# A layer with two long convolutions: PE's loop taken over groups 4 to 31, keys and values in one place each, fixed places for the second convolution's tiles

## What is computed

```
q, k, v = u Wq + bq, u Wk + bk, u Wv + bv          # per channel, over 512 positions
k  = causal_conv(k, k_kernel) + k_D * k            # first convolution, taps 512 long
kv = k * v
y  = causal_conv(kv, ssm_kernel) + D * kv          # second convolution
y  = (y * q) Wo + bo
x  = layernorm(u + y)
h  = square(relu(x W_fc));  d = h W_proj
s  = spikes of five steps of a leaky integrator driven by d, over 5
out = layernorm(x + s)
```

## Time and profile before

| | us |
|---|---|
| median of three runs | 869.58 |
| the profiled execution | 871.54 |
| its span | 869.4 |
| PE busy | 744.9 |
| DVE busy | 703.2 |
| ACT busy | 529.6 |
| POOL busy | 391.1 |

### The profile page before, as it was taken

The page is one execution under the profiler, slowest core; times in us unless marked ns, Lnnn a source line. Parts: engine busy times, 40 slices in busy tenths (PEclk is TensorE's granted clock), DMA queues, the critical chain, the costliest instruction groups (busy, mean ns, idle before and its releaser), DMA issues.

```text
span 869.4 us, 26708 instructions
## 1 busy us (share of the span) xinstructions
PE 744.9 (86%) x11392; PEld 547.4 (63%) x11392; DVE 703.2 (81%) x1100; ACT 529.6 (61%) x625; POOL 391.1 (45%) x307
## 2 busy tenths in 40 slices
PE   0068879999999798775499999999999999999993
PEld 0068879999999798775355555555555455555541
DVE  6896737877878757675569999999999999999885
ACT  2383748878877757665255556665556655566661
POOL 0332212223222212221475667866668766687542
PEclk9999969999999989776699999999999999999997
DMA  9994859999999867773000110011110111101001
GB/s 336 342 245 127 198 136 215 223 232 230 221 240 229 193 156 150 156 191 99 25 25 1 49 48 25 24 48 48 48 48 0 48 48 48 48 3 47 25 25 48
DMA packets 55580, 101.01 MB, mean 116 GB/s; under 512 B 5729, under 2 KB 41441, under 8 KB 53601
## 3 DMA queue, kind: packets, MB, share of 16 engines
q1 hardware_dynamic: 54144, 97.94, 43.9%
q10 hardware_dynamic: 1376, 2.23, 0.7%
HBM read 89.92 MB, written 27.01 MB: 134 GB/s over the span
## 4 chain that ended last, share of the span: by engine, by line
PE 44%; DVE 21%; POOL 17%; issue 11%; ACT 4%; DMA 1%; SPq 0%; POOLq 0%; DVEq 0%; ACTq 0%
PE ps L763 18%; POOL arena L687 14%; PE ps L741 13%; DVE arena L1238 7%; PE ps L874 5%; PE ps L881 5%; DVE u_maxima L975 2%; DVE arena L1195 2%; DVE arena L1235 2%; PE ps L855 2%; DVE arena L1214 2%; DVE arena L1220 2%; ACT arena L506 1%; PE ps L836 1%; DVE arena L1206 1%
## 5 line engine op out<-in xcount | busy, mean ns | idle before, releaser
L741 PE MATMUL ps<-arena 128*128 128x96 f16 x3072 | 143.3, 210 | 62.8 <-DVE arena L1028 51.1
L687 POOL TENSOR_TENSOR arena<-arena 128x512 f16<-128x512 f32 x128 | 178.6, 1426 | 14.9 <-ACT arena L570 14.3
L741 PEld LDWEIGHTS ps<-arena 128*128 128x128 f16 x3072 | 138.4, 100 | 64.7 <-issue 58.7
L881 PE MATMUL ps<-arena 128*128 128x512 f16 x768 | 173.2, 379 | 2.7 <-POOL arena L687 2.7
L874 PE MATMUL ps<-arena 128*128 128x512 f16 x768 | 170.8, 379 | 0.9 <-issue 0.9
L763 PE MATMUL ps<-arena 128*128 128x64 f16 (+2 forms) x5088 | 148.8, 184 | 25.9 <-issue 13.3
L763 PEld LDWEIGHTS ps<-arena 128*128 128x128 f16 x5088 | 145.4, 99 | 27.8 <-issue 20.7
L652 POOL TENSOR_TENSOR arena<-arena 128x512 f16<-128x512 f32 x32 | 37.8, 1182 | 245.3 <-ACT arena L526 245.3
L1227 DVE TENSOR_TENSOR arena<-arena 128x512 f32<-128x512 f32 x128 | 138.4, 1136 | 9.6 <-POOL arena L687 7.8
L566 ACT ACTIVATE arena<-ps,read_factor 128x512 f32<-128x512 f32 x128 | 88.0, 687 | 79.4 <-PE ps L874 62.7
L881 PEld LDWEIGHTS ps<-arena 128*128 128x128 f16 x768 | 73.9, 98 | 90.4 <-POOL arena L687 9.5
(11 more groups left out here) (108 smaller groups left out, 901.1 us busy)
## 6 DMA issues: line engine op xcount, KB each, us to landing
arena<-kpad_dram SPq DMA_DIRECT2D x166, 256.0 KB, 5.3
kpad_dram<-ksplit_dram SPq DMA_DIRECT2D x64, 256.0 KB, 6.1
qy<-in_uT SPq DMA_DIRECT2D x8, 1024.0 KB, 17.4
arena<-in_u SPq DMA_DIRECT2D x16, 512.0 KB, 4.1
out<-arena SPq DMA_DIRECT2D x16, 512.0 KB, 3.0
qy<-kpad_dram SPq DMA_DIRECT2D x22, 256.0 KB, 6.5
arena<-in_k SPq DMA_DIRECT2D x2, 512.0 KB, 4.8
ksplit_dram<-arena ACTq DMA_DIRECT2D x2, 512.0 KB, 3.3
```

Source lines behind the costliest of these rows:

```text
L687: nc.gpsimd.tensor_tensor(h16[:, 1, f], h_square[:, f % 4], h16[:, 0, f], ALU.subtract).then_inc(h_lo, 1)
L741: last = nc.tensor.matmul(o, u16[:, x, t, tok:tok + P], wcur[:, w, t], start=(k == 0), stop=(k == 3 * DT - 1))
L881: return nc.tensor.matmul(PD[:, t], wp16[:, w, f, t * P:(t + 1) * P], h16[:, h, f], start=first, stop=last)
```

## The change

The second convolution's windows get four fixed places, two halves for even and two for odd groups, in the same array as the first convolution's; `slot_of` and its table go. To make room, keys and values are kept in one 4 by 4 array of blocks each (quarter by group). A chunk is read out by group; a group's four blocks are free once it is used, and the same quarter of the next chunk is written into just these, transposed. So the chunks with even numbers are written into one contiguous run, and those with odd numbers into four separate blocks, by four instructions of 128 elements for the keys and four for the values in place of one of 512 each. kv gets a buffer of its own, `kv`, and is no longer stored over v; the factor that `times_v` applied moves into the reading of the values. The values may be written only after `times_v(g)` has used the block, so their reading moves behind it (`read_values`). The split keys have one buffer in place of two.

With places that depend on the parity of the group alone, PE's loop runs over the groups 4 to 31, fourteen iterations; an outer If leaves the projection out in the last two. The groups 0 to 3 and conv2(31) are written out. In the second phase `wo` and `bo_b` lie behind `yT`, and the staging area begins at 20 KB. The zeroing of the windows' upper partitions is regrouped: it is done before group 0 for all four places of the second convolution, and the separate memsets of before, for the query place, the token place and the late place, go.

```diff
         u16 = part(64, F16, "p (a t n) -> p a t n", a=2, t=DT)
-        kv_at = at[0]
-        kbuf = part(16, F32, "p (r q n) -> p r q n", r=2, q=GPC)
-        vbuf = part(16, F32, "p (r n) -> p r n", r=2)
+        kbuf = part(8, F32, "p (a b n) -> p a b n", a=GPC, b=GPC)
+        vbuf = part(8, F32, "p (a b n) -> p a b n", a=GPC, b=GPC)
+        kv = part(2, F32)
...
-        k16 = part(4, F16, "p (r a n) -> p r a n", r=2, a=2)
+        k16 = part(2, F16, "p (a n) -> p a n", a=2)
...
-        T = part(6 * 8, F16, "p (k c a n) -> p k c a n", k=6, c=HG, a=2)
-        at[0] = 48 * KB
-        T2 = part(2 * 8, F16, "p (k c a n) -> p k c a n", k=2, c=HG, a=2)
-        T3 = qy[:, (NC - 2) * CH * COL:].bitcast(F16).rearrange("p (k c a n) -> p k c a n", k=2, c=HG, a=2)
-        T4 = u16[:, :, :, 0:TOK // GPC].rearrange("p k t (c n) -> p k t c n", n=L)
-
-        step_st = kv16[:, 0, 0, 0:P]
+        t_at = at[0]
+        T = part(8 * 8, F16, "p (k c a n) -> p k c a n", k=8, c=HG, a=2)
+        step_st = k16[:, 0, 0:P]
...
+        def group_in(buf, s):
+
+            nth = s % GPC
+            return buf[:, :, nth] if s % PAIR < GPC else buf[:, nth]
+
         def keys_of(s):
-
-            n = s % GPC * (GC // GPC)
-            return kbuf[:, s % PAIR // GPC, :, n:n + GC // GPC].rearrange("p q (m b) -> p q m b", b=4)
+            return group_in(kbuf, s).rearrange("p q (m b) -> p q m b", b=4)
...
-        def windows2_of(g, half):
-            place, nth = slot_of(g, half)
-            if place == TOKENS:
-                return T4[:, nth].rearrange("p t (c a) n -> p t (c a) n", a=2)
-            t = (T[:, 4 + nth], T2[:, nth], T3[:, nth])[place]
-            return t.rearrange("p (t c) a n -> p t (c a) n", t=2)
+        def windows2_of(s, half):
+            return T[:, 4 + s % 2 * 2 + half].rearrange("p (t c) a n -> p t (c a) n", t=2)
...
-                convolve(0, PC1[:, s % 2], lambda a, ch: k16[:, s % 2, a, ch * COL:(ch + 1) * COL],
-                         lambda half, c, a: windows1_of(s, half)[:, c, a], g + 1, c1_half)
+                for half in range(2):
+                    pe.wait_ge(c1_copied[half], g + 1)
+                    convolve(half, PC1[:, s % 2], k16, lambda c, a: windows1_of(s, half)[:, c, a], c1_half)
...
-            def pair_of_steps(first, nth):
-
-                g = first + 2 * nth
-                with pe.If(nth % 2 == 0):
-                    project(first % GPC, g + GPC)
-                with pe.Else():
-                    project((first + 2) % GPC, g + GPC)
-                conv1(first, g)
-                conv2(first - 1, g - 1)
-                with pe.If(nth % 2 == 0):
-                    pe.wait_ge(wcur_ready, nth + (first + 1) // 2 + 2)
-                    project((first + 1) % GPC, g + 1 + GPC)
-                with pe.Else():
-                    project((first + 3) % GPC, g + 1 + GPC)
-                conv1(first + 1, g + 1)
-                conv2(first, g)
-
-            LOOPED = range(3, QUERY_UNTIL + 1)
-            for g in range(LOOPED.start):
+            def pair_of_steps(nth):
+
+                g = FIRST + 2 * nth
+                with pe.If(nth < (NG - GPC - FIRST) // 2):
+                    with pe.If(nth % 2 == 0):
+                        pe.wait_ge(wcur_ready, nth + FIRST // 2 + 2)
+                        project(0, g + GPC)
+                    with pe.Else():
+                        project(2, g + GPC)
+                conv1(0, g)
+                conv2(1, g - 1)
+                with pe.If(nth < (NG - GPC - FIRST) // 2):
+                    with pe.If(nth % 2 == 0):
+                        project(1, g + 1 + GPC)
+                    with pe.Else():
+                        project(3, g + 1 + GPC)
+                conv1(1, g + 1)
+                conv2(0, g)
+
+            FIRST = GPC
+            for g in range(FIRST):
                 step(g)
-            with pe.Fori(0, len(LOOPED) // 2) as nth:
-                pair_of_steps(LOOPED.start, nth)
-            for g in range(LOOPED.stop, NG):
-                step(g)
+            with pe.Fori(0, (NG - FIRST) // 2) as nth:
...
+            def read_scaled(s, buf, quarter, r, chunk, banks):
+
+                src, factor, bias_s = tiles_of(banks, s), read_factor[:, 2 * s:2 * s + 1], bias_of(chunk, s)
+                if r == 0:
+                    return nc.vector.scalar_tensor_tensor(buf[:, quarter].rearrange("p b (d m) -> p (b d) m", d=G),
+                                                          src, factor, bias_s, ALU.mult, ALU.add)
+                for n in range(GPC):
+                    some = slice(n * G, (n + 1) * G)
+                    last = nc.vector.scalar_tensor_tensor(buf[:, n, quarter].rearrange("p (d m) -> p d m", d=G),
+                                                          src[:, some], factor, bias_s[:, some], ALU.mult, ALU.add)
+                return last
...
+            def read_keys_queries(quarter, r, n, chunk, banks=PA):

                 dve.wait_ge(proj, n + 1)
-                tiles = banks.rearrange("p i (b x) -> p x (i b)", b=4)
-                for s, dst in ((0, kbuf[:, r, quarter]), (1, quarter_of(vbuf[:, r], quarter)),
-                               (2, quarter_of(qy[:, bass.ds(chunk * CH * COL, CH * COL)], quarter))):
-                    if s == 2 and quarter == 0 and chunk >= NC - 2:
-                        g0, h0 = USES[QUERY, chunk - (NC - 2)][-1]
-                        dve.wait_ge(c2_half, 2 * g0 + h0 + 1)
-                    bb = bias_b[:, bass.ds(chunk, 1), s].rearrange("p c d -> p (c d)").to_broadcast([P, CH, NI * 4])
-                    src = tiles[:, s * CH:(s + 1) * CH]
-                    if s == 0:
-                        nc.vector.scalar_tensor_tensor(dst.rearrange("p (d m) -> p d m", d=CH), src, read_factor[:, 0:1], bb,
-                                                       ALU.mult, ALU.add)
-                    else:
-                        last = nc.vector.tensor_tensor(dst.rearrange("p (d i) b -> p d i b", i=NI),
-                                                       src.rearrange("p d (i b) -> p d i b", b=4),
-                                                       bb.rearrange("p d (i b) -> p d i b", b=4), ALU.add)
-                last.then_inc(proj_read, 1)
+                read_scaled(0, kbuf, quarter, r, chunk, banks)
+                dst = quarter_of(qy[:, bass.ds(chunk * CH * COL, CH * COL)], quarter)
+                nc.vector.tensor_tensor(dst.rearrange("p (d i) b -> p d i b", i=NI),
+                                        tiles_of(banks, 2).rearrange("p d (i b) -> p d i b", b=4),
+                                        bias_of(chunk, 2).rearrange("p d (i b) -> p d i b", b=4), ALU.add)
+
+            def read_values(quarter, r, chunk, banks=PA):
+                read_scaled(1, vbuf, quarter, r, chunk, banks).then_inc(proj_read, 1)
                 if quarter == GPC - 1 and chunk + 1 < NC:

                     dve.wait_ge(ld_wnext, 16 * (chunk + 1))
                     nc.vector.tensor_copy(wcur, wnext).then_inc(wcur_ready, 2)
...
                 if more:
-                    if s % GPC == 0 and not (first and s == 0):
-
-                        dve.wait_ge(kv_lo, g)
-                    read_projection(s % GPC, (s // GPC + 1) % 2, g + GPC, chunk + s // GPC + 1)
+                    dve.wait_ge(k_lo, g + 1)
+                    read_keys_queries(s % GPC, (s // GPC + 1) % 2, g + GPC, chunk + s // GPC + 1)
                 times_v(s, g, base + (s // GPC + 1) * GPC)
+                if more:
+                    dve.wait_ge(kv_ready, g + 1)
+                    read_values(s % GPC, (s // GPC + 1) % 2, chunk + s // GPC + 1)
```

More of the change, by code:

```diff
@@ L158, in build @@
         wp16 = part(8, F16, "p (a t n) -> p a t n", a=2, t=FT)
[L159 to L160 removed]
+        at[0] = 20 * KB
         stage_at = at[0]
@@ L167, in build @@
         yT = part(4, F32, "p (t n) -> p t n", t=DT)
+        wo = part(2, F32, "p (t n) -> p t n", t=DT)
+        bo_b = part(1, F32)
         sum1 = part(4, F32, "p (i n) -> p i n", i=NI)
@@ L351, in load_windows @@
                 if conv:
-                    place, nth = slot_of(g, half)
-                    for n in range(PIECES if place == TOKENS else 1):
-                        windows, size = windows2_of(g, half)[0:QP], run
-                        if place == TOKENS:
-                            windows = windows[:, n].rearrange("p c n -> p (c n)")
-                        else:
-                            windows, size = windows.rearrange("p t c n -> p (t c n)"), row
-                        sp.dma_start(windows, bass.AP(first.tensor, first.offset + n * run,
-                                                      [[ROWS - QP // NCOPY, NCOPY], [-1, QP // NCOPY], [1, size]])
-                                     ).then_inc(t2_in[2 * place + nth], 16)
+                    sp.dma_start(windows2_of(g, half)[0:QP].rearrange("p t c n -> p (t c n)"),
+                                 bass.AP(first.tensor, first.offset,
```

(31 more changed lines are left out.)

157 lines of the change are left out of this document (54 added, 103 removed).

## The result

The changed kernel takes 863.41 us (median of five runs, 860.08 to 864.36) against 869.75 before (five runs); the ratio of the runs is 0.9908, with a 95% interval of 0.9881 to 0.9936. It is faster by 0.9%, some 6 to 8 us where 15.35 were forecast, and 863.4 lies above the range of 850 to 861. The profiled executions stand 863.41 (span 861.2) against 871.54 (span 869.4): 8.2 us of span to be explained.

The account below looks back on a forecast made before the run. PE bounded the looped steps; written-out steps 21 to 27 starved for instructions, 28 to 31 also waited for ACT. 15.05 + 4.3 - 2.2 - 1.4 - 0.4 = 15.35 us saved, forecast 854.2 us, range 850 to 861.

Parts of the forecast that it names:

- part 1: Steps 21 to 27 go into PE's loop at 9.25 us each: 15.05 us saved, lower end 9.9.
- part 4: More branches in PE's loop cost 0.1 us per iteration, 1.4 us over fourteen; ends 0 and 4.2.
- part 5: DVE's reading of odd chunks in eight pieces, values hidden in its conv2 wait: costs 0.4 us, ends 0 and 3.
- part 3: Step 3, written out ahead of PE's loop, costs 2.2 us at the feeding rate; upper end 5.6.
- the rival that DVE becomes the bound: In steps reading an odd chunk, eight PSUM reads at 0.66 us cost 32 us: 886 us; chance 0.03.
- Parts 2 and 6: Steps 28 to 31 save 4.3 us, ends 3.28 and 7.7; single buffers of split keys and kv cost nothing.
- Part 6: One buffer each of split keys and kv costs nothing; 1.3 us in seven steps if the cover went.
- Part 7: Fixed window places, loads still two deep, larger memset ahead of group 0 in DVE's wait for PE: costs nothing.

## Why the prediction was off

The mechanism was right: written-out code starves PE, the loop is kept, and in the steps 21 to 27 q8 moved no packet and the clock stood at 1.00, as part 1 said; they took 9.43 us each in place of 9.25, which parts 4 and 5 explain. Four terms were mis-sized, and one of them hid a wait that I had not seen. Of the 7.1 us that are missing in the span, 4.5 lie at the start (2.1 of part 5, 1.9 of part 3, 0.5 that were there before conv1(0)), 2.1 in the loop (part 4 above all) and 1.0 in the tail; the second phase gave 0.5 back.

*Part 5, "the values go into that hole".* True for every step but step 0, where PE projects again straight behind conv1(0). I read the hole from a step in the middle of the loop and did not lay the new order over the first step. The wait that I had put at nothing is 1.95 us long, and by the kernel with the loop from 3 the start is 2.1 us longer for it (1.8 to 2.1 by the starts of conv1(0) and conv1(1)). This is the step that failed as mechanism; it alone does not make the miss. In the loop a piece took 0.26 to 0.28 us for the forecast 0.30, `kv_ready` less than the 0.1 taken, and the rival that DVE becomes the bound did not come. The 0 to 0.2 us by which the weight copy was to come late rest on no row: twice it held PE up, by 0.42 and 0.47 us, because it took 0.94 us and not 0.246. PE's waits for DVE in the loop are 1.4 us in all, where the part had 0.4; all three lie at a turn of the loop, where the other turns show a gap as long without them.

*Part 3, "I take 2.2".* One more written-out step cost 3.4 to 3.8 us, and 4.1 in the changed kernel with the outer If, inside the ends of 0.1 and 5.6. So the 6.7 us by which step 5 ends later are 2.1 of late values, 4.1 of this step and its If, and 0.5 by which conv1(0) already starts later (78.21 against 77.67). It starts between 77.3 and 78.5 in all kernels in which the fourth projection ran at the low clock, so the 0.5 is not the change's as far as can be told.

*Part 4, "0.1 each".* The nested If cost 0.26 us an iteration, 2.9 us over the eleven of the steps 6 to 27, by the kernel without it; the forecast was 1.4 for all fourteen, its upper end 4.2. The gap at the turn was 0.42 to 0.51 in place of 0.23 to 0.31. The last 0.06 us a step, between 9.31 without the If and 9.25 before, lies at the turns and in two waits of 0.37 us for the weight copy.

*Parts 2 and 6.* 3.3 us against 4.3. The start and the end of this stretch in the kernel after (line 459 is ACT's split of the next group's keys, line 464 its copy of windows):

```profile
353.66 1.13 DVE L985 SCALAR_TENSOR_TENSOR arena<-ps,read_factor,arena 128x128 f32<-128x128 f32 x4
354.82 0.63 ACT L459 ACTIVATE arena<-arena 128x512 f16<-128x512 f32 x1 [0.53 <-DVE arena L985]
355.47 1.70 ACT L464 ACTIVATE arena<-arena 64x1792 f32<-64x1792 f32 x1
357.31 6.83 PE L700 MATMUL ps<-arena 128*128 128x64 f16 x192 [2.65 <-ACT arena L464]
...
392.47 3.66 PE L700 MATMUL ps<-arena 128*128 128x64 f16 x96 [4.32 <-ACT arena L469]
```

As forecast conv2(31) still waits for ACT's copy (4.32 us). What came in place of the rest is the wait ahead of conv1(28), 2.65 us where it was 1.44. It has two causes of 1.2 us together. Ahead of `times_v(27)` stand a shifted copy, the four pieces of the keys and the queries' reading, so that it is 0.8 us late where part 5 had up to 0.3; moving the copy took 0.7 us off. And group 28 begins a new chunk, so ACT's split of its keys waits for the values' reading: 0.53 us, which go on through the copy at 355.47 to PE. Part 6 had seen this wait and took it to be covered by the 2.8 us that POOL has in the middle of the loop; ahead of conv1(28) there is no projection to cover it.

*Part 7* costs nothing that shows, and of part 6 nothing else does: no wait on `k_lo` or `kv_lo` appears among DVE's.

## What to carry to other kernels

Where an engine waits for "issue", count its code against the instruction queue's packets in that stretch: a stream that eats a block faster than the queue brings one is bound by its own length, and a loop whose body is kept removes that bound, up to a size that has to be tried. The first pass is fed like straight code, so start the loop as early as its waits allow; each step written out ahead of it cost some 2 to 4 us here. Where work is moved into a hole, look for the step that hasn't got the hole: the first and the last. And before two kernels' starts are compared, look whether they were alike ahead of the edit: here 1.6 of 3.1 us had been won before it.

## What the runs showed of the hardware

PE keeps a loop body of 1536 matmul and weight instructions, some 98 KB at 16 KB for 256 of them, through taken branches over up to 24 KB (no packet on q8 from 147.1 to 392 us in the changed kernel), and not one of 2304, some 147 KB (46 packets in four iterations). The sizes are estimates from the packets. A block of 16 KB came every 4.2 to 5.3 us beside a DMA share of 0.70 to 0.79 (8 packets in 33.3 us and 15 in 79.8 before; 46 in 213 with four steps; 54 in 271 without a loop), and 11.2 to 11.4 us a step followed from it. A turn with one If level cost up to 0.31 us (0.36 in the loop from 2), with two 0.42 to 0.51. An address instruction in PE's stream cost 0.06 us. DVE took 0.26 us from one read of 128 elements of PSUM to the next and 0.66 for 512. A copy of 384 f16 elements took 0.25 us, and 0.94 where it stood behind four such short reads of late values; the cause is open.
